# Routing attention on one core: three bfloat16 pieces of queries and keys in two halves of the array, all key gathering on VectorE

## The reference

```
xq = round(min(1, |x|) * 7) / 7 ;  x = conv3x3(xq, sign(W) * mean|W|) + b          # 64 -> 64 channels
q, k, v = split(layernorm(x) @ wqkv + bqkv)                                        # 8 heads of 8
regions: 7x7 regions of 8x8 positions (R = 49, 64 positions each)
idx = top_k(mean_region(q) @ mean_region(k).T, 4)                                  # 4 regions for each region
kg, vg = k[idx], v[idx]                                                            # 256 keys and values
scores = einsum('brqhd,brkhd->brhqk', q, kg) / sqrt(8) ;  attn = softmax(scores)
x = x + (attn @ vg) @ wo + bo
x = x + gelu(layernorm(x) @ w1 + bm1) @ w2 + bm2
```

## Time and profile before

| | |
|---|---|
| median of three runs | 5526.65 us |
| profiled execution: span from first to last instruction | 5568.0 us |
| one pair (98 steps), the eighth | 328.84 us |
| busy: PE / DVE / ACT / POOL | 84% / 62% / 59% / 49% |
| mean granted TensorE clock | 0.909 |
| DMA | 487.33 MB, 627124 packets |

### The profile page before, as it was taken

One profiled execution on the slowest core, in us unless ns is written; L12 is line 12 of the kernel. 1 busy time (PEld: TensorE's weight loads), 2 busy tenths in 40 slices (PEclk: granted clock), 3 DMA queues, 4 the chain that ended last, 5 costly groups with the idle time before them and its releaser, 6 DMA issues.

```text
span 5568.0 us, 230234 instructions
## 1 busy us (share of the span) xinstructions
PE 4677.0 (84%) x68754; PEld 3217.0 (58%) x68754; DVE 3447.6 (62%) x7969; ACT 3285.4 (59%) x6282; POOL 2747.0 (49%) x9656
## 2 busy tenths in 40 slices
PE   2388888888889888888888888888888888888888
PEld 1265565656556565565656656565565656556564
DVE  2266666666666666666666666666566666667665
ACT  1156556565665656556565665656556565665656
POOL 1245455454544545445454554545455454554553
PEclk8589999998998999889989999989899999989999
DMA  1333343333333333333333423333343333323311
GB/s 53 102 98 92 83 109 76 100 77 96 102 77 98 84 95 91 82 103 80 94 83 91 111 72 103 81 96 92 79 109 79 96 81 102 100 75 102 84 40 33
DMA packets 627124, 487.33 MB, mean 88 GB/s; under 512 B 483792, under 2 KB 613968, under 8 KB 615536
## 3 DMA queue, kind: packets, MB, share of 16 engines
q10 hardware_dynamic: 335360, 205.62, 16.4%
q1 hardware_dynamic: 290416, 265.73, 16.2%
HBM read 262.38 MB, written 208.73 MB: 85 GB/s over the span
## 4 chain that ended last, share of the span: by engine, by line
PE 45%; DMA 18%; issue 10%; SPq 7%; ACT 7%; DVE 5%; DVEq 3%; POOL 2%; ACTq 2%; POOLq 1%
DMA max_d<-tr 11%; PE ps L988 9%; PE ps L1002 7%; PE ps L1019 7%; PE ps L881 4%; DMA qm<-qk_d 3%; PE ps L938 3%; DMA xin<-in_x 3%; DVEq L223 2%; DVE mx L724 2%; SPq L327 2%; PE ps L949 2%; PE ps L901 2%; ACT hid L813 2%; PE ps L974 2%
## 5 line engine op out<-in xcount | busy, mean ns | idle before, releaser
L724 DVE TENSOR_REDUCE mx<-ps 128x4 f32<-128x1024 f32 x1568 | 1921.7, 1226 | 1702.3 <-PE ps L988 1354.0
L832 ACT ACTIVATE pt<-ps 128x512 f32<-128x512 f32 x3136 | 1694.3, 592 | 869.2 <-PE ps L1002 814.4
L506 POOL COPY vg<-vs 64x64 f32 x6272 | 1526.5, 243 | 782.0 <-POOL kg L490 576.7
L988 PE MATMUL ps<-kg,qm 96*128 96x256 f32 x6272 | 1336.2, 338 | 386.6 <-DVE mx L724 127.3
L490 POOL CAST kg<-ks 96x128 fp32r x3136 | 851.0, 297 | 1511.6 <-PE ps L1002 1156.6
L988 PEld LDWEIGHTS ps<-kg,qm 96*128 96x128 f32 x6272 | 946.8, 202 | 1053.6 <-issue 889.5
L1002 PE MATMUL ps<-qm,kg 97*128 97x256 f32 x6272 | 1119.8, 301 | 178.8 <-ACT pt L832 102.3
L1019 PE MATMUL ps<-pt,vg 128*32 128x64 f32 x50176 | 1091.4, 231 | 0.0
L1002 PEld LDWEIGHTS ps<-qm,kg 97*128 97x128 f32 x6272 | 926.2, 203 | 252.2 <-ACT pt L832 164.8
L1019 PEld LDWEIGHTS ps<-pt,vg 128*32 128x32 f32 x50176 | 826.1, 115 | 224.2 <-issue 34.8
L643 DVE CAST kg<-ks 96x128 fp32r x3136 | 625.6, 241 | 126.2 <-issue 123.5
(11 more groups left out here) (109 smaller groups left out, 3866.7 us busy)
## 6 DMA issues: line engine op xcount, KB each, us to landing
qk_d<-stg SPq DMA_DIRECT2D x224, 448.0 KB
qm<-qk_d ACTq DMA_DIRECT2D x1792, 42.0 KB
ks<-qk_d ACTq DMA_DIRECT2D x96, 784.0 KB, 6.2
vs<-v_d ACTq DMA_DIRECT2D x64, 784.0 KB, 6.7
xin<-in_x SPq DMA_DIRECT2D x119, 224.0 KB
xi_d<-xi SPq DMA_DIRECT2D x112, 224.0 KB
qk_d<-stg SPq DMA_DIRECT2D x112, 224.0 KB
max_d<-tr SPq DMA_DIRECT2D x1568, 2.0 KB
```

What stands on the lines that cost most here:

```text
L506: j = pool.tensor_copy(dst.rearrange("p j (e x) -> p j e x", e=2)[:, :, :, 0:HD], vs[place(m)[0]][rows, bass.ds(region, 1), :].rearrange(" ...
L724: v.tensor_reduce(mx[h % 2][:].rearrange("p (g j e) -> p g j e", g=2, j=2)[:, :, :, 0], ps[:, 0:2, :].rearrange("p g (j k) -> p g j k", j= ...
L832: act.activation(pt[m % 2][:, c], ps[:, 2 + c, :], ACT.Exp, scale=float(HD) ** -0.5).then_inc(S["pt_ready"], 1)
L988: i = pe.matmul(ps[:, g, 256 * j:256 * j + 256], qm[c % 2][0:NP3, t, g, 2 * j:2 * j + 2, :].rearrange("p h t -> p (h t)"), kg[slot][0:NP3, ...
```

## The change

Queries and keys are split into three bfloat16 pieces (high, middle, low) instead of two float32r pieces used three times. Six products of pieces stay (6 x 8 = 48 rows for a head). A head no longer shares rows with three others: heads 0 to 3 use array rows 0 to 47, heads 4 to 7 rows 64 to 111 (row 48 and 112 hold the maxima against -1). `scores` is 8 matmuls of 64 columns, each in a quarter of the array (row half by column half), 256 bfloat16 moving; `turned` is 16 matmuls of 128 columns, 64 moving, alternating between the row halves. `qm` needs no zeros and is filled by 2 DMAs instead of 8; the keys of an image by 12 small ones instead of 3. The maxima and their row are bfloat16, `tr` is a ring of 7, and the reduction no longer waits for a landing; the transpose waits for one seven steps back. DVE gathers the keys of all four regions, as 32-bit words, with 4 copies; POOL gathers only values, and takes the low piece of each strip (`lowest`). ACT writes the middle piece. `turned` now waits for both exponentials of the step before at its start, and both its signals come at its end.

```diff
-        qk_d = dram("qk_d", (PAIRS, 2, 2 * C, 3, NT))
+        q_d = dram("q_d", (PAIRS, C, PARTS, 2, NT), BF16)
+        k_d = dram("k_d", (PAIRS, C, 3, 2, NT), BF16)
...
-        qm = [sb(f"qm{i}", [128, NW, NG, HG, RT], F32R) for i in range(2)]
-        kg = [sb(f"kg{i}", [128, NG, TOPK, RT], F32R) for i in range(RING)]
+        qm = [sb(f"qm{i}", [128, HG, NW, RT], BF16) for i in range(2)]
+        kg = [sb(f"kg{i}", [128, HG, TOPK, RT], BF16) for i in range(RING)]
...
-            if t in (3, 4, 5) and live((c + 1) * NW, kind):
+            if t in (3, 4) and live((c + 1) * NW, kind):
...
                 if live(h, kind):
                     v.wait_ge(S["sm_full"], T + 1)
-                    if live(h - 2, kind):
-                        v.wait_ge(hopped[h % 2], (p * R + (h - 2) // 2 + 1) * 16)
...
-                for k, region in enumerate(regions(v, regs, m, 0, 2)):
-                    j = v.tensor_copy(kg[slot][0:NP3, :, k, :],
-                                      ks[place(m)[0]][0:NP3, :, bass.ds(region, 1), :].rearrange("p g o t -> p g (o t)"))
+                for k, region in enumerate(regions(v, regs, m, 0, TOPK)):
+                    j = v.tensor_copy(kg[slot][:, :, k, :].bitcast(U32),
+                                      ks[place(m)[0]][:, :, bass.ds(region, 1), :].rearrange("p h o t -> p h (o t)").bitcast(U32))
...
+                    if off in (6, 7):
+                        i = off - 6
+                        act.wait_ge(S["res_ready"], n * 2 + i + 1)
+                        act.activation(stg[k % 2][:, 1, i], res[:, i], ACT.Copy).then_inc(S["m_ready"], 1)
...
+                        pool.tensor_tensor(stg[k % 2][:, 2, i], res[:, i], stg[k % 2][:, 1, i], ALU.subtract).then_inc(S["l_ready"], 1)
...
-                pe.wait_ge(S["kp_ready"], T + 1)
...
-                for g in range(NG):
-                    for j in range(2):
-                        i = pe.matmul(ps[:, g, 256 * j:256 * j + 256],
-                                      qm[c % 2][0:NP3, t, g, 2 * j:2 * j + 2, :].rearrange("p h t -> p (h t)"),
-                                      kg[slot][0:NP3, g].rearrange("p k t -> p (k t)"), start=True, stop=True)
+                settled(pe)
+                for j in range(2):
+                    for g in range(NG):
+                        d = slice(64 * g, 64 * g + HROW)
+                        for e in range(2):
+                            i = pe.matmul(ps[64 * e:64 * e + 64, g, 256 * j:256 * j + 256], qm[c % 2][d, 2 * j + e, t, :],
+                                          kg[slot][d, 2 * j + e].rearrange("p k t -> p (k t)"), start=True, stop=True)
...
+                    pe.wait_ge(S["pt_ready"], T * 2)
                 for b in range(2):
...
+                    for h in range(HG):
+                        for g in range(NG):
+                            d = slice(64 * g, 64 * g + HROW + 1)
+                            i = pe.matmul(ps[:, 2 + g, 256 * b + 64 * h:256 * b + 64 * h + 64],
+                                          kg[slot][d, h, 2 * b:2 * b + 2, :].rearrange("p k t -> p (k t)"),
+                                          qm[c % 2][d, h, t, :], start=True, stop=True)
+                            if b and h == HG - 1:
+                                i.then_inc(S["st_full"], 1)
```

More of the change, by code:

```diff
@@ L51 @@
 ROUTE_AT = 62
-A_LOAD, B_LOAD = 70, 6
-QK_DMAS, V_DMAS = 3, 4
-KV_DMAS = 5
+A_LOAD, B_LOAD = 70, 3
+QK_DMAS, V_DMAS = 4, 4
+KV_DMAS = 2 * PARTS + 2
+K_PIECE = (0, 0, 0, 1, 1, 2)
+Q_DMAS = 2
 def p_item(h):
-    return [(k, h - P_AT - P_EVERY * k) for k in range(NW) if 0 <= h - P_AT - P_EVERY * k <= 10]
+    return [(k, h - P_AT - P_EVERY * k) for k in range(NW) if 0 <= h - P_AT - P_EVERY * k <= 11]
 def f_item(h):
@@ L132, in build @@
         xh = sb("xh", [128, ST])
-        stg = sb("stg", [128, 2, 2, ST], F32R)
+        stg = [sb(f"stg{i}", [128, 3, 2, ST], BF16) for i in range(2)]
+        res = sb("res", [128, 2, ST])
         vstg = sb("vstg", [128, 4, 2, VW])
@@ L177, in build @@
         idx_loaded = [sem(f"idx_loaded{i}") for i in range(2)]
-        hopped = [sem(f"hopped{i}") for i in range(2)]
+        qk_staged = [sem(f"qk_staged{i}") for i in range(2)]
+        hopped = [sem(f"hopped{i}") for i in range(RING)]
         row_ready = [sem(f"row_ready{i}") for i in range(RING)]
@@ L256, in loads @@
                     settled(eng)
-                queries(eng, p + (c + 1) // 14, (c + 1) % 14, [(g, h) for g in range(NG) for h in range(HG)][(t - 3) * 3:(t - 2) * 3])
+                queries(eng, p + (c + 1) // 14, (c + 1) % 14, t - 3)
             if kind == "loop":
@@ L323, in stage, with part @@
                         sp.dma_start(xi_d[bass.ds(q, 1), k].rearrange("o p n -> (o p) n"), xi[:].bitcast(F32)).then_inc(S["xi_stored"], 16)
-                    def part(slot, rows, low):
-                        dst = qk_d[bass.ds(q, 1), :, 0:rows, slot, cut].rearrange("o i c n -> (o c) i n")
-                        sp.dma_start(dst, stg[0:rows, low].bitcast(F32)).then_inc(S["qk_staged"], 16)
+                    low = stg[k % 2]
+                    def part(out, slots, src):
+                        dst = out[bass.ds(q, 1), :, slots, :, cut].rearrange("o c s i n -> (o c) (s i) n")
+                        sp.dma_start(dst, src.rearrange("p s i n -> p (s i) n")).then_inc(qk_staged[k % 2], 16)
                     def value(i, half):
@@ L347, in stage @@
                         value(1, 1)
+                        sp.wait_ge(S["l_ready"], q * (2 * NW) + 2 * k + 2)
+                        settled(sp)
+                        part(k_d, slice(0, 3), low[C:2 * C])
+                    if off == 11:
+                        part(q_d, slice(0, 3), low[0:C])
+                        part(q_d, slice(3, 5), low[0:C, 0:2])
             def route(q, i):
@@ L558, in before @@
                             quantize(q * NW + k, NW if q and k == 0 else None, None, k, off)
+                    if not q:
+                        for h in range(P_AT, ROUTE_AT + 6):
+                            lowest(0, h, None)
                 pool.wait_ge(S["xq_done"], 1 + 2 * NW)
@@ L561, in before @@
                     fetch(0, m)
-                for m in range(AHEAD):
-                    keys(0, m, "lead")
             steps(pool, step, before)
```

157 lines of the change are left out of this document (77 added, 80 removed).

## The result

The changed kernel took 5861.1 us (median of four runs, 5859.3 to 5870.9), the kernel before 5534.7 in the same comparison. The ratio is 1.060, 95% interval 1.057 to 1.064: 6% slower, where I had forecast 5300 us and a gain of 4%. The profiled execution spans 5869.0 us.

What follows compares the result with a forecast made beforehand. PE (84% busy) was the suspect, tied in quiet steps with the scores-reduction loop; DVE or ACT set others. Cycles -5.4 and -1.8, stalls -7: -14.2 us a pair, times 16 = -227, so 5300 us from 5526.65; range 5080 to 5600.

Steps and rivals of the forecast that it cites:

- Stalls: -7: Irregular stalls, 18.6 us a pair: 5 gained from query waits, 2 from the reduction's landing waits; -7 us a pair.
- the six-step stretch: Six steps of item `p`, 18.10 us, seven times a pair: forecast to change by -0.77 us each, -5.4 a pair.
- The 4.18 us step: Step of item `p` where DVE waits 2.20 us for a landing of the maxima; forecast to gain 0.70 us.
- ACT and POOL, at nothing: ScalarE's and POOL's changed work priced at zero; exponential loop 1.9 us, under the quiet step's 2.14.
- PE's part: TensorE: `scores` -0.23 us, `turned` zero, new change of shape +0.12; sum -0.11 us a step.
- my low bound: `turned` on PE: about 0.2 us less if a weight load fell under the 64 moving columns.
- DVE's part: VectorE: two more key copies +0.30 us (bounds +0.14 and +0.66); quiet steps fall from 2.22 to 2.14 us.
- The copy train: Rival: DVE's copies between reduction and transpose set the pace, +0.66 instead of +0.30 us; 5690 us, chance 0.13.
- halves that do not overlap: Rival: `turned`'s row halves do not overlap, +0.34 us on 53 PE-filled steps; 5735 us, chance 0.12.
- Better overlap: Rival: loads hide under moving columns, -0.2 us more on 53 steps; 5130 us, about 5050 with more; chance 0.15.
- The row's case: Rival: the wait for the maxima's row replaces the landing wait entirely, nothing of the stalls goes; 5490 us, chance 0.13.
- P: Theory from the follow-up experiments, not the prediction: TensorE's shorter work lowers its clock, which costs the rest.

Runs made afterwards that it cites:

- both lags: Changed kernel, read-back issued two steps after its maxima instead of one, second product four steps behind the first instead of three: 5506.6 us, ratio 0.990.
- the halved gathering: Changed kernel with VectorE gathering the keys of only two of the four regions: 5857.8 us, ratio 1.053.
- the order bank by bank: Changed kernel, second product's sixteen matmuls ordered one row half after the other, signal and wait for each bank apart: 5974.8 us, ratio 1.073.
- the cheap read-back: Changed kernel, read-back fetching only 64 of the 512 maxima as one piece: 5673.9 us, ratio 1.022.
- relaxing one alone: Changed kernel, only the read-back of a step's maxima moved, to two steps after it instead of one: 6088.9 us, ratio 1.096.
- the other alone: Changed kernel, only the second product moved, to four steps behind the first instead of three, other work one step later: 5802.7 us, ratio 1.045.
- the lags: Kernel before, with read-back two steps behind and second product four behind: 5515.3 us, ratio 0.994.
- its staging moved too: Changed kernel, read-back two steps behind, second product four, staging on ScalarE's queue: pieces only 5378.3 us, ratio 0.969; values too 5364.4 us, 0.969.

## Why the prediction was wrong

**The failed step is "Stalls: -7".** I wrote that the row "takes over most of that wait" and took 2 us more a pair as gain. I had named the serial chain through SP and priced a rival in which "Nothing of the stalls goes", at 5490 us, as the worst it could do. What I never priced was the read-back's own issue, although the order of SP's queue showed its shape change from `1x512` to `2x4x64`. It went from 0.23 to 0.53 us, 1568 times (865 us of issue in all against 389): 476 us more on a queue that waited for its own landings already. The staging of the pieces, unpriced as well, adds some 104 us to it (297 against 193). Raising the read-back's issue in the old kernel cost 158 us, lowering it in the new one returned 187, and relieving the chain with both lags returned the whole loss.

The reduction's wait and the queries' did go (451 us). But the row's wait rose from 78 to 620 us, PE and its loads together. By the rows it shows in the six-step stretch, for which I had forecast 18.10 - 0.77 = 17.33 us and which took 19.65. The 4.18 us step gave back 0.96 (I had 0.70); the one of 2.22 us, which I had at 2.14, took 4.41. The pair took 22 us more and not 14.2 less.

The signs that I had set down did not catch this. The reduction has no DMA wait, the wait for queries is under 30 us, and `turned` waits for its row over 100 us: all three came true. I had put no upper bound on the last.

**Second, "ACT and POOL, at nothing".** I worked out 1.9 us for the loop turned, exponentials, turned and called it covered at 2.14. In a step where ScalarE does little else it is covered: `turned` starts at 3107.65, its exponentials end at 3109.17, and the next `turned` at 3109.48 did not wait for them. Yet the wait for ScalarE grew from 267 to 591 us. It falls in steps where ScalarE has other work ahead of the exponentials; some three quarters of PE's own share of it (241 us) follow the Gelu activations (L833) and a table load (L205):

```profile
3094.52 1.28 ACT L205 ACT_TABLE_LOAD   x1
3095.81 1.09 ACT L852 ACTIVATE pt<-ps 128x512 f32<-128x512 f32 x2
3096.95 0.61 PE L1025 MATMUL ps<-qm,kg 49*128 49x64 bf16 x16 [2.24 <-ACT pt L852]
```

What this wait costs in time is not shown: the run that shortened it also lengthened the product. It also stood in the run with both lags (547 us), which had lost nothing against the kernel before.

**PE's part was right in kind and too small.** I forecast 0.48 us for `scores` and 0.6 to 0.7 for `turned`; they took 0.41 and 0.41. PE-filled steps lost 0.27 and 0.29 us where I had 0.11. All 16 loads of 128 bfloat16 columns fit into 0.29 us, where I had set 0.056 a load in each half (0.45 us for eight). By its time `turned` is nearer to my low bound. The Trainium skill (TensorE: Matmul & The Clock Gate, Weight-path perf modes) has a fast weight load for 128 columns of a type other than fp32, which I had cited for that bound. One load of `turned` lasts 95 ns, near the 102 of the earlier trace rows and half of the 203 before, and 16 of them fit into 0.29 us because they overlap; whether the fast load is at work the rows do not tell.

**DVE's part was right.** Four copies in 0.66 (0.6 to 0.75 forecast), and no cost where they are covered. From one reduction to the next it took 1.88 us (3107.77 to 3109.65) instead of 2.14: I had added reduction, copies and transpose end to end, and the rows show that each starts before the one ahead has ended (copies at 3108.91, reduction until 3109.00).

**The rivals.** The copy train (5690) and halves that do not overlap (5735) gave times nearer to the truth than the forecast did, but by mechanisms that are refuted: by the 0.66 and the halved gathering, by the 0.41 and the order bank by bank. That they had the sign right was luck. (The two also count PE-filled steps differently, 23 and 53; with 53 the copy train's price is some 50 us lower.) Better overlap (5130) had PE's part right and the time most wrong. The row's case had the right place and the wrong price: it took the chain as untouched, and the change had lengthened it.

**The clock.** "Wrong: ... a mean clock below 0.85" came true: 0.821. Behind the wait of 1.84 us at 3242.20 the granted clock fell to 0.50, the 1.2 GHz level, for the next two steps; `attended` took 1.08 us in them instead of 0.65:

```profile
3244.36:3246.48 2.12, 2.12 (x58) 1.47 (x58) 1.43 (x4) 1.99 (x4) 0.26 (x2) 0.50 0.03 8
```

By these rows a part of what the row's wait costs is paid through the clock. But the mean is 0.834 with the cheap read-back and 0.844 with both lags, which is no slower than the kernel before at 0.909. A low clock came with every version of the changed kernel and did not prevent a gain; P by itself is not the cause of the 6%. How much the clock costs, and how much of the way from 5507 us to the forecast 5300 it takes, was not measured.

## What to carry to other kernels

Price every DMA issue on the queue that carries the step's round trip, not only its bytes: here 0.3 us more at the issue of a 1 KB read-back, in every step, outweighed all that TensorE gained. When an in-order queue waits for its own landings, its pace and the latency of each item can bind together; here relaxing one alone cost 4%, the other alone gained 1%, and both together gained 6% of the changed kernel's time. Before speeding up the busiest engine, ask which serial chain has the same period, and relieve that in the same change: the kernel before had 0.6% to gain from the lags, the changed one 6%, and 8% with its staging moved too.

## What was not expected of the hardware

One contiguous piece issues in 0.23 to 0.24 us on SP (2048, 1024 or 128 bytes alike; medians); two pieces of 512 bytes take 0.50, eight of 128 bytes 0.53, while the query load of 192 pieces of 896 bytes takes 0.32 on ScalarE's queue. What sets this is open. Sixteen matmuls of 49 rows, 128 columns and 64 moving bfloat16 columns, alternating between two row halves, take 0.41 us from first start to last end, no longer than eight with 256 moving columns in four quarters.
